# First turn of an attention and graph kernel: one bias on its own semaphore, x loaded and used in halves, and another order of the setup

## What is computed

```
q, k, v = x @ Wq.T + bq, x @ Wk.T + bk, x @ Wv.T + bv          # 8 heads of 32
p = softmax(where(mask, q @ k.T * SCALE, -1e9))                # 6 fixed masks, 2 from adj
h = layernorm(x + (p @ v) @ Wo.T + bo)
Wh = h @ W[head].T + bW;  e = Wh @ attn[head]                  # 4 heads
A = tanh(where(adj, e @ Wh.T, 0));  ha = concat(relu(A @ Wh)) @ A_w.T
hf = h @ fc_w.T;  c = sigmoid(hf @ g1_w.T + ha @ g2_w.T + gbias)
out = layernorm(h + hf * c + ha * (1 - c))
```

## Time and profile before

| | |
|---|---|
| median of 3 runs | 1116.5 us (1112.35 to 1117.24) |
| profiled execution | 1114.91 us, span 1113.1 us |
| PE busy | 1090.0 us, 98% of the span |
| DVE, ACT, POOL busy | 711.7, 542.1, 281.3 us |
| mean granted clock of the span | 0.992 |
| chain that ended last | PE 96% |

### The profile page before, as it was taken

The page is one execution under the profiler, slowest core; times in us unless marked ns, Lnnn a source line. Parts: engine busy times, 40 slices in busy tenths (PEclk is TensorE's granted clock), DMA queues, the critical chain, the costliest instruction groups (busy, mean ns, idle before and its releaser), DMA issues.

```text
span 1113.1 us, 25068 instructions
## 1 busy us (share of the span) xinstructions
PE 1090.0 (98%) x10018; PEld 911.4 (82%) x10018; DVE 711.7 (64%) x1353; ACT 542.1 (49%) x958; POOL 281.3 (25%) x247
## 2 busy tenths in 40 slices
PE   7999999999999999999999999999999999999995
PEld 5878888888888888888888888888788888888774
DVE  6666765757666666765757666575765666676543
ACT  3654463635536364563735546363563635445351
POOL 1533222232312313222232312213221231322200
PEclk8999999999999999999999999999999999999998
DMA  7000100001010000100001010000100100010000
GB/s 258 2 22 22 40 23 21 19 21 39 21 38 22 20 19 21 39 21 20 22 20 37 21 39 21 20 19 21 39 21 20 40 20 19 21 40 3 1 19 19
DMA packets 26699, 32.58 MB, mean 29 GB/s; under 512 B 4400, under 2 KB 23344, under 8 KB 26288
## 3 DMA queue, kind: packets, MB, share of 16 engines
q1 hardware_dynamic: 26672, 32.19, 8.6%
HBM read 23.80 MB, written 8.39 MB: 29 GB/s over the span
## 4 chain that ended last, share of the span: by engine, by line
PE 96%; DVE 1%; DMA 1%; ACT 1%; issue 0%; SPq 0%; POOL 0%; POOLq 0%; DVEq 0%
PE bank L380 17%; PE bank L381 17%; PE bank L385 17%; PE bank L372 8%; PE bank L374 8%; PE bank L373 8%; PE bank L575 5%; PE bank L598 4%; PE bank L489 3%; PE bank L502 3%; PE bank L520 2%; PE bank L645 1%; PE bank L545 1%; PE bank L408 1%; DMA bias_v<-in_bv 1%; PE bank L420 1%
## 5 line engine op out<-in xcount | busy, mean ns | idle before, releaser
L840 ACT ACTIVATE cat_hi<-bank 128x512 fp32r<-128x512 f32 x128 | 76.6, 598 | 127.0 <-PE bank L385 127.0
L805 ACT ACTIVATE T<-bank 128x512 f32<-128x512 f32 x128 | 76.6, 599 | 102.6 <-PE bank L385 100.8
L936 DVE SCALAR_TENSOR_TENSOR cat_lo<-bank,cat_hi 128x512 fp32r<-128x512 f32 x128 | 86.5, 686 | 38.9 <-ACT cat_hi L840 36.8
L936 DVE SCALAR_TENSOR_TENSOR U_lo<-bank,U_hi 128x512 fp32r<-128x512 f32 x128 | 78.0, 682 | 50.5 <-ACT U_hi L834 50.5
L380 PE MATMUL bank<-hT_hi,g_lo 128*128 128x512 f32 x256 | 102.9, 402 | 0.0
L381 PE MATMUL bank<-hT_hi,g_hi 128*128 128x512 f32 x256 | 99.9, 390 | 0.0
L381 PE MATMUL bank<-U_hi,wt_hi 128*128 128x512 f32 x256 | 99.8, 390 | 0.0
L380 PE MATMUL bank<-U_hi,wt_lo 128*128 128x512 f32 x256 | 99.8, 390 | 0.0
L372 PE MATMUL bank<-cat_lo,aw_hi 128*128 128x512 f32 x256 | 99.6, 389 | 0.0
L373 PE MATMUL bank<-cat_hi,aw_lo 128*128 128x512 f32 x256 | 99.6, 389 | 0.0
L374 PE MATMUL bank<-cat_hi,aw_hi 128*128 128x512 f32 x256 | 99.6, 389 | 0.0
(11 more groups left out here) (154 smaller groups left out, 2743.3 us busy)
## 6 DMA issues: line engine op xcount, KB each, us to landing
y<-in_x SPq DMA_DIRECT2D x16, 512.0 KB, 3.6
out<-res SPq DMA_DIRECT2D x16, 512.0 KB, 3.0
x_raw<-in_xT SPq DMA_DIRECT2D x15, 512.0 KB, 3.3
W_nat<-in_Wn SPq DMA_DIRECT2D x1, 1028.0 KB, 6.1
attn_nat<-in_attn SPq DMA_DIRECT2D x1, 1024.0 KB, 8.6
adjS_u<-in_adjS SPq DMA_DIRECT2D x32, 32.0 KB, 2.7
raw_A<-in_AwT SPq DMA_DIRECT2D x1, 1024.0 KB, 8.0
x_second<-in_xT SPq DMA_DIRECT2D x1, 512.0 KB, 9.6
```

The source lines that it names most:

```text
L805: take(act.activation(T[:, n % DC, n // DC, :], bank[:], ACT.Copy), "B", f"T{n}", g)
L840: act.activation(cat_hi[:, n, :], bank[:], ACT.Relu).then_inc(cat_hi_ready, 1)
L936: return dve.scalar_tensor_tensor(out=out, in0=bank, scalar=bias, in1=hi.bitcast(F32), op0=op, op1=ALU.subtract)
```

## The change

Turn 0 is reordered on all engines, and its beginning is loaded differently. bias_v gets its own semaphore and is loaded after raw_o. ACT issues the first half of x (the first 128 of 256 features) and the biases of q and k itself, ahead of its first copy; SP loads the other half. ACT splits x in halves and PE's first queries wait for each half by itself. The masks and attn_nat are loaded ahead of raw_v. Both halves of v and both of attention are computed in one go each, project follows four G products, W_transposed stands behind project, h_T before gate_weights. Aw is split by ACT in two halves, and POOL takes x_low ahead of Aw's low part. In the loop only two counter increments on SP are added (`carried` once for each wait).

```diff
--- before.py
+++ after.py
@@ -31,8 +31,8 @@
-LAST_IN_BANK = {False: ("probT1", "probT2", "probT3", "v1"), True: ("probT0", "probT1", "probT2", "probT3")}
-SPLIT_ORDER = ("G0", "G1", "G2", "G3", "G4", "G5", "G6", "W0", "W1", "W2", "W3", "G7", "FC")
+LAST_IN_BANK = {False: ("probT2", "probT3", "v1"), True: ("probT0", "probT1", "probT2", "probT3")}
+SPLIT_ORDER = ("G0", "G1", "G2", "G3", "G4", "G5", "G6", "G7", "W0", "W1", "W2", "W3", "FC")
...
 FIRST = listed("Q0:0 Q1:1 K0:2 K1:3 score0:0 score1:1 score2:2 score3:3 M0:4 M1:5 M2:6 M3:7 M4:4 M5:5 M6:6 M7:7 v0:0 "
-               "probT0:1 probT1:2 G0:4 G1:5 G2:6 G3:7 probT2:3 probT3:0 v1:1 G4:4 G5:5 G6:6 attn0:2 attn1:3 "
-               "W0:7 W1:4 W2:5 W3:6 y0:0 y1:1 G7:7 q0:2 q1:3 FC:4 FF:5 hT0:0 hT1:1 k0:2 k1:3")
+               "probT0:1 probT1:4 v1:2 G0:5 G1:6 probT2:3 probT3:0 G2:7 attn0:1 attn1:4 G3:2 G4:5 G5:6 G6:7 y0:0 y1:3 "
+               "G7:2 W0:5 W1:6 W2:7 W3:1 q0:4 q1:2 hT0:0 hT1:3 FC:5 FF:6 k0:7 k1:1")
...
+        first_in, first_hi = sem("first_in"), sem("first_hi")
...
             load(raw_q[:], wq, early_in[0])
-            xT_load(0)
+            load(x_raw[:, 1, :], xT[0, :, 1, :], xT_in)
             load(raw_k[:], wk, early_in[1])
-            load(bias_q[:], bq, bias_in)
-            load(bias_k[:], bk, bias_in)
             load(W_nat[:], Wn, nat_in)
+            load(raw_m[:], masks, mask_in)
+            load(attn_nat[:], attn, attn_in)
             load(raw_v[:], wv, early_in[2])
-            load(attn_nat[:], attn, attn_in)
-            load(raw_m[:], masks, mask_in)
-            load(bias_v[:], bv, bias_in)
             adjS_load(0)
             for half_ in range(2):
                 load(eye2[half_ * S:half_ * S + S], eye[0:S, 0:S], eye_in)
             load(ident[:], eye, ident_in)
             load(raw_o[:], wo, early_in[3])
+            load(bias_v[:], bv, bias_v_in)
             x_load(0)
...
-                    carried(sp)
+                        carried(sp)
...
+            def first_queries():
+                for c in range(DC):
+                    bank = claim(pe, "A", f"q{c}", 0)
+                    cols = slice(c * P, c * P + P)
+                    for k in range(DC):
+                        if c == 0:
+                            pe.wait_ge((first_hi, x_hi_ready)[k], 1)
+                            if k == 0:
+                                pe.wait_ge(early_hi, 1)
+                        pe.matmul(bank[:], Wq[0][:, k, cols], x_hi[:, k, :], start=k == 0, stop=False)
+                        if c == 0 and k == 0:
+                            pe.wait_ge(weights_ready, 1)
+                        pe.matmul(bank[:], Wq[1][:, k, cols], x_hi[:, k, :], start=False, stop=False)
+                    if c == 0:
+                        pe.wait_ge(x_ready, 1)
+                    for k in range(DC):
+                        ins = pe.matmul(bank[:], Wq[0][:, k, cols], x_lo[:, k, :], start=False, stop=k == DC - 1)
+                    filled(ins, "A", f"q{c}", 0)
...
                 if B is None:
                     warm_up()
-                    queries(0)
+                    first_queries()
                     keys(0)
                     scores(0)
                     M1_products(range(H2 * DC))
                     values(0, 0)
                     probs_T(0, range(2))
-                    G_products(range(4))
+                    values(0, 1)
+                    G_products(range(2))
                     probs_T(0, range(2, JB))
-                    values(0, 1)
-                    G_products(range(4, 5))
-                    attention(0, range(1))
-                    G_products(range(5, 7))
-                    attention(0, range(1, DC))
-                    W_transposed()
+                    G_products(range(2, 3))
+                    attention(0, range(DC))
+                    G_products(range(3, 7))
                     project(0)
                     G_products(range(7, H2 * DC))
+                    W_transposed()
                     queries(1)
+                    h_T(0)
                     gate_weights()
-                    h_T(0)
                     keys(1)
                     return
...
+            def first_loads():
+                act.dma_start(x_raw[:, 0, :], xT[0, :, 0, :]).then_inc(first_in, 16)
+                act.dma_start(bias_q[:], bq).then_inc(bias_in, 16)
+                act.dma_start(bias_k[:], bk).then_inc(bias_in, 16)
+
             def early():
-                for n, (w, raw) in enumerate(((Wq, raw_q), (Wk, raw_k))):
-                    act.wait_ge(early_in[n], 16)
-                    act.activation(w[0][:], raw[:], ACT.Copy).then_inc(early_hi, 1)
-                    if n == 0:
-                        x_split(0)
+                act.wait_ge(early_in[0], 16)
+                act.activation(Wq[0][:], raw_q[:], ACT.Copy).then_inc(early_hi, 1)
+                act.wait_ge(first_in, 16)
+                act.activation(x_hi[:, 0, :], x_raw[:, 0, :], ACT.Copy).then_inc(first_hi, 1)
+                act.wait_ge(xT_in, 16)
+                act.activation(x_hi[:, 1, :], x_raw[:, 1, :], ACT.Copy).then_inc(x_hi_ready, 1)
+                act.wait_ge(early_in[1], 16)
+                act.activation(Wk[0][:], raw_k[:], ACT.Copy).then_inc(early_hi, 1)
 
...
-            def late():
+            def late(n):
+
                 act.wait_ge(late_in, 16 * 2)
-                for w, raw in ((Aw, raw_A), (G2, raw_g2)):
-                    act.activation(w[0][:], raw[:], ACT.Copy).then_inc(late_hi, 1)
+                to, raw = ((Aw[0][:, 0:4, :], raw_A[:, 0:4, :]), (Aw[0][:, 4:8, :], raw_A[:, 4:8, :]), (G2[0][:], raw_g2[:]))[n]
+                act.activation(to, raw, ACT.Copy).then_inc(late_hi, 1)
...
-                    act.wait_ge(bias_in, 16 * 3)
+                    act.wait_ge(bias_in, 16 * 2)
...
             def attention(g):
+                if not later(g):
+                    act.wait_ge(bias_v_in, 16)
...
                 if B is None:
+                    first_loads()
                     early()
                     queries(0)
+                    masks_in()
                     value_weight()
-                    masks_in()
                     keys(0)
                     M1_copies(range(1))
                     exps(0, 0)
@@ -871,24 +901,28 @@
                     exps(0, 1)
                     M1_copies(range(3, 6))
                     out_weight()
+                    M1_copies(range(6, 7))
                     exps(0, 2)
-                    M1_copies(range(6, H2 * DC))
+                    M1_copies(range(7, H2 * DC))
+                    late(0)
                     values(0, 0)
                     exps(0, 3)
-                    late()
                     probs_T(0, range(2))
-                    G_high(range(4))
+                    values(0, 1)
+                    x_split(1, x_second)
+                    G_high(range(2))
                     probs_T(0, range(2, JB))
-                    values(0, 1)
-                    G_high(range(4, 5))
-                    x_split(1, x_second)
+                    G_high(range(2, 3))
+                    attention(0)
+                    G_high(range(3, 5))
+                    late(1)
                     G_high(range(5, 7))
-                    attention(0)
+                    late(2)
+                    G_high(range(7, H2 * DC))
                     W_high()
-                    G_high(range(7, H2 * DC))
                     queries(1)
+                    h_T(0)
                     fc_high()
-                    h_T(0)
                     h_high(0)
                     gate_high()
                     keys(1)
...
             def early():
                 early_low(0, Wq, raw_q)
+                dve.wait_ge(first_hi, 1)
+                dve.tensor_tensor(x_lo[:, 0, :], x_raw[:, 0, :], x_hi[:, 0, :].bitcast(F32), ALU.subtract)
                 dve.wait_ge(x_hi_ready, 1)
-                dve.tensor_tensor(x_lo[:], x_raw[:], x_hi[:].bitcast(F32), ALU.subtract).then_inc(x_ready, 1)
+                dve.tensor_tensor(x_lo[:, 1, :], x_raw[:, 1, :], x_hi[:, 1, :].bitcast(F32), ALU.subtract) \
+                   .then_inc(x_ready, 1)
                 early_low(1, Wk, raw_k)
...
                 if B is None:
                     early()
                     shifted_weights()
-                    early_low(2, Wv, raw_v)
                     shift(0, 0)
                     shift(0, 1)
                     mask(0)
+                    early_low(2, Wv, raw_v)
                     softmax_rest(0)
                     early_low(3, Wo, raw_o)
-                    G_low(range(1))
                     shifted_fc()
-                    G_low(range(1, 7))
+                    G_low(range(3))
                     attention(0)
-                    W_low()
+                    G_low(range(3, 7))
                     residual(0)
                     G_low(range(7, H2 * DC))
+                    W_low(range(2))
                     new_h(0)
```

(22 more changed lines are left out.)

## The result

The changed kernel takes 1112.78 us (median of 20 runs, 1111.29 to 1116.31), the kernel before 1115.59 (20 runs, 1112.35 to 1117.24). The ratio is 0.9979, 95% interval 0.9971 to 0.9986: faster, by 2.3 us. (The medians lie 2.8 apart; the ratio is formed within each round and is the better measure.) The profiled execution took 1112.86, span 1110.7 (before 1114.91 and 1113.1). The ratios use fast executions alone: one of experiment 5 (1357.5 us), one of experiment 7 (2782.8) and one of the kernel before beside experiments 1, 3, 5 and 7 (1553.3) ran slow and are left out of them.

The account below looks back on a forecast made before the run. PE work was taken to bound everything behind T0; T0 at 54.2 instead of 58.0 gains 3.8 us, giving 1111.1 from the profiled 1114.9 or 1112.7 against the median; forecast 1111.5, range 1107.5 to 1115.5.

Parts of the forecast that it names:

- x in halves worth nothing, covered by the warm-up: First q passes in turn 0: halves of x gain 0, bounds +0.3 and -1.0 us, since warm-up matmuls hold PE.
- q drained at 8.3; raw_v is late next and lands at 12.9: ACT's drains in turn 0: q's first at 8.3, k's behind raw_v at 12.9; scores start at 15.15, 1.6 us earlier.
- Clock stays full with a gap of 2.8 us: PE between k and scores: idleness shrinks from 4.4 to 2.8 us, so the clock does not fall to half.
- the rival with chance 0.13: Clock falls anyway after PE's 2.8 us gap before the scores: gain only 1.9 us, 1113 us; chance 0.13.
- Softmax chain: Turn 0 from scores to attention: first shift at 16.35, M1 done at 24.2, attention starts at 33.0.
- From attention to T0 21.2 us: PE's setup from attention at 33.0 through project, h_T, gate weights and keys(1) to T0's first matmul at 54.2.
- POOL's 0.2: POOL ahead of root_1, behind aw_lo and g_lo: no slack left, 0.2 us charged.
- PE's gap ahead of h_T: PE in the setup: with gate weights moved behind h_T, it idles 1.4 us before h_T.
- Rival 4: POOL's queue: aw_lo and g_lo ending after 44.5 delay root_1 and T0; slower, 1117 us at 6 us late; chance 0.07.
- T0 3.8 earlier: First matmul of T0, at the end of the setup: 54.2 instead of 58.0, 3.8 us earlier.
- Everything behind T0 is PE work that the change leaves alone: The loop after the setup: PE busy 69.73 of 70 us a turn, so time won before T0 comes off the end.
- Rival 3: PE's gaps at attention and before h_T double, or the loop's first turn gives gain back: 0.5 to 1.5, 1114; chance 0.13.

Follow-up runs that it names:

- experiment 5: Kernel before with only the new front (bias_v's own semaphore, x in halves, new load order, masks before Wv on ACT): 1113.41 us, ratio 0.9981.
- experiment 7: Changed kernel with x loaded and split whole again, loaded by SP, and queries(0) as before: 1112.35 us, ratio 0.9981.
- experiments 1: Changed kernel with three fp32 matmuls on zeros between keys(0) and scores(0): 1109.53 us, ratio 0.9958.
- 3: Changed kernel with ACT draining k ahead of the copy of Wv's high part: 1112.61 us, ratio 0.9968.
- experiments 10 and 11: Changed kernel with three matmuls on zeros before scores(0), gate_weights ahead of h_T: 1108.33 us; 11 adds balanced banks and split attention: 1109.56 us.
- experiment 8: Changed kernel with two tiles of turn 0 in other banks, giving fill counts as in the kernel before: 1111.46 us, ratio 0.9954.

## Why the prediction came out as it did

- *x in halves worth nothing, covered by the warm-up*: the value is right, 0.9981 without and 0.9979 with. The cover isn't shown to be the warm-up: in experiment 7, without halves, k ends 0.9 later (0.3 of it because the warm-up ended later), and it is the wait for raw_v that hides it. The three issues on ACT cost what was said (table load 0.73 before, 2.15 after) and are hidden too. (bias_v was the tenth load on SP, not the ninth; nothing hangs on it.)
- *q drained at 8.3; raw_v is late next and lands at 12.9*: right, and the step that carries the forecast. Drained at 8.03, landed at 3.61 + 9.89 = 13.50. The term was mis-sized by 0.6: the scores start 1.1 earlier than in the earlier trace rows and not 1.6. Counting the bytes ahead in the queue gave the landing within 5%.
- *Clock stays full with a gap of 2.8 us*: wrong, the first step that failed. The gap was 3.6, and the clock fell to 0.50 for 6.8 us, which cost 2.2 at T0 (experiment 1). A gap of 2.8 would not have kept it either: it fell behind 2.7 (experiment 7) and behind 1.1 (experiment 3), though for 3.4 us only. This is the rival with chance 0.13, and its time of 1113 is nearly the one measured; there too part is luck, since it put T0 1.9 earlier, where it was 2.6, and knew nothing of the turn. The Trainium skill's "TensorE: Matmul & The Clock Gate", Part 1, has the clock go by how busy PE has been and gives idleness as the state in which it is throttled. Idleness alone doesn't sort the traces here: the clock stayed full behind 1.3 us of it (experiment 1) and fell behind 1.1 (experiment 3) and 1.4 (experiments 10 and 11), each time while PE was on score passes or M1. The measurement decides.
- *Softmax chain*: the shift at 17.11 (16.35 said), M1 done at 27.95 (24.2), attention at 35.07 (33.0). The clock accounts for all of the 2.1 us there: experiment 1, at the same start of the scores, has attention at 32.86. The late start of the scores (0.5) was made up on the way, 17.2 us to attention for the 17.9 said.
- *From attention to T0 21.2 us*: 20.2. POOL's 0.2 was not needed (POOL waited 0.3 for the moments), PE's gap ahead of h_T was 1.0 for 1.4. Rival 4 stayed where it was put, one step from deciding.
- *T0 3.8 earlier*: 2.6. With the clock as in experiment 1's profile it would have been 4.8.
- *Everything behind T0 is PE work that the change leaves alone*: false, the second step that failed, and hidden. The turn of the loop grew by 0.12 us, 0.11 of it through the bank counts (experiment 8). Rival 3, "gain eaten", allowed for a loss in the first turn of the loop, not for one in every turn.

The forecast of 1111.5 came near because errors of both signs met. On the span, the clock took 2.2 us and the loop 1.5; against that stand 1.0 on the way from attention and 1.3 in turns 1 and 2 and at the end, most of the latter from a standstill that the profile of the kernel before happened to have. That makes 2.4 of the 3.8. (Against the median of twenty executions of the kernel before, 1115.6, a gain of 3.8 would have been 1111.8.)

## What to carry to other kernels

When a wait is taken away, look for the next load in the same engine's order, by bytes ahead of it in the queue; that found the new bound here. Before trusting that a shorter gap keeps the clock, ask what PE does on either side of it: a few matmuls on zeros in the gap are a cheap test, and in the old kernel they were worth about as much as the whole reordering. They held the clock in four profiles of six: look at the clock of more than one execution before you rely on them. And compare the period of the loop before and after a change of the prologue: its counts reach into the loop through every wait that counts from them.

## What was not expected of the hardware

- Half clock followed 1.1 us of idleness and 1.9 us of 32 x 64 passes (experiment 3). With 2.7 us of dense matmuls on zeros ahead of 1.3 to 1.4 us of idleness and the same passes it stayed full in one profile (experiment 1) and fell in two (10 and 11).
- Half clock lasted either 3.4 or 6.8 us in these ten profiles, and a gap of 3.5 us was followed by 3.4 (experiment 8), one of 3.6 by 6.8 (the changed kernel).
- PE stood still for 2.4 us in the middle of 128 short passes in four of the profiled executions (experiments 3, 7, 8 and 10), each time from 0.2 to 0.3 us after a fetch of instructions had begun; in others, with a fetch some microseconds ahead of the passes, it didn't. In turn 1 of the kernel before it stood 1.1 us in the scores, 1.1 us after a fetch had begun. What decides in which executions it happens stays open.
- A DMA issue took ACT 0.41 to 0.47 us, SP 0.40 to 0.48 for most, and ACT's table load stood behind the three issues (2.15 for 0.73).
- Two waiting instructions in front of attention's first pass instead of one go with 0.11 us a turn (0.33 for 0.22 from the last product's start).
